# Gated attention and routed experts on one core: a new order of the steps ahead of the expert loop

## The reference

```
x = x + tanh(g_xattn) * attention(layernorm(x), ctx)
    # inside: layernorm of both again, q, k, v, softmax(q k^T / 16), v, Wo
n = layernorm(x)
w = softmax(n @ gate_w + gate_b)                # 8 experts
values, chosen = top_k(w, 2)
hidden = relu(n @ w1[e] + b1[e])                # 256 -> 1024
y[e] = hidden @ w2[e] + b2[e]                   # 1024 -> 256
x = x + tanh(g_ffn) * sum(values * y[chosen])
```

## Time and profile before

| what | value |
|---|---|
| median of 3 runs | 595.58 us (593.59 to 598.76) |
| the profiled execution, its own time | 594.17 us |
| its span, first to last instruction | 592.4 us |
| mean granted TensorE clock in it | 0.916 |
| TensorE busy | 513.9 us (87%) |
| ScalarE busy | 425.9 us (72%) |
| VectorE busy | 396.0 us (67%) |
| GpSimd busy | 276.6 us (47%) |

### The profile page before, as it was taken

One profiled execution on the slowest core, in us unless ns is written; L12 is line 12 of the kernel. 1 busy time (PEld: TensorE's weight loads), 2 busy tenths in 40 slices (PEclk: granted clock), 3 DMA queues, 4 the chain that ended last, 5 costly groups with the idle time before them and its releaser, 6 DMA issues.

```text
span 592.4 us, 15755 instructions
## 1 busy us (share of the span) xinstructions
PE 513.9 (87%) x4747; PEld 426.8 (72%) x4748; DVE 396.0 (67%) x1148; ACT 425.9 (72%) x1077; POOL 276.6 (47%) x292
## 2 busy tenths in 40 slices
PE   6958547566989998989999989999999999999991
PEld 3535325335878887768888877888999998999981
DVE  3359669787876666778666777876655665665660
ACT  2649688777766675867677756887888888888870
POOL 3110334843672223968732367885775233233232
PEclk8985575567999999999999999999999999999997
DMA  6999503233633224234332232534433332332221
GB/s 170 368 381 347 195 1 98 84 120 126 180 87 63 37 29 118 30 74 103 88 60 39 65 81 38 120 93 76 85 59 52 56 47 47 56 49 46 38 28 18
DMA packets 47633, 57.07 MB, mean 96 GB/s; under 512 B 6855, under 2 KB 43197, under 8 KB 47423
## 3 DMA queue, kind: packets, MB, share of 16 engines
q1 hardware_dynamic: 32223, 36.60, 20.3%
q0 software_dynamic: 14064, 18.55, 18.1%
q10 hardware_dynamic: 1264, 0.93, 0.5%
HBM read 33.19 MB, written 24.49 MB: 97 GB/s over the span
## 4 chain that ended last, share of the span: by engine, by line
PE 45%; DVE 10%; issue 8%; ACT 6%; POOL 3%; DMA 2%; ACTq 1%; DVEq 1%; SPq 0%; POOLq 0%
PE hid L1815 8%; PE hid L1819 7%; PE bank L1837 6%; PE bank L1839 6%; PE bank L1838 6%; PE hid L1818 4%; PE hid L1816 4%; ACT pool L924 3%; DVE pool L1468 3%; POOL xs L599 2%; PE bank L1796 2%; PE bank L1657 2%; PE bank L1675 1%; DVE pool L1483 1%; POOL out_dram L682 1%
## 5 line engine op out<-in xcount | busy, mean ns | idle before, releaser
L682 POOL DMA_INDIRECT out_dram<-pool,idx x71 | 115.4, 1625 | 196.1 <-DVE pool L1483 156.0
L924 ACT ACTIVATE pool<-hid,b1s 128x128 f32<-128x128 f32 x568 | 168.9, 374 | 12.7 <-PE hid L1819 4.7
L1815 PE MATMUL hid<-pool,w1h 128*128 128x256 f16 x568 | 155.4, 274 | 6.5 <-DVE pool L1468 3.5
L1837 PE MATMUL bank<-w2h,pool 128*128 x568 | 154.8, 273 | 4.3 <-issue 3.7
L1819 PE MATMUL hid<-pool,w1h 128*128 128x256 f16 x568 | 155.4, 274 | 0.0
L1839 PE MATMUL bank<-w2h,pool 128*128 x568 | 154.8, 273 | 0.0
L1838 PE MATMUL bank<-w2l,pool 128*128 x568 | 154.8, 273 | 0.0
L1468 DVE TENSOR_TENSOR pool<-hid,pool 128x512 f32<-128x512 f32 x142 | 96.5, 689 | 68.6 <-ACT pool L924 68.5
L1818 PE MATMUL hid<-pool,w1l 128*128 128x128 f16 x568 | 124.8, 220 | 0.0
L1816 PE MATMUL hid<-pool,w1l 128*128 128x128 f16 x568 | 124.8, 220 | 0.0
L933 ACT ACTIVATE pool<-pool 128x512 f16<-128x512 f32 x142 | 89.9, 637 | 36.0 <-DVE pool L1468 35.6
(11 more groups left out here) (276 smaller groups left out, 745.7 us busy)
## 6 DMA issues: line engine op xcount, KB each, us to landing
pool<-xs SPq DMA_DIRECT2D x71, 132.5 KB, 2.3
pool<-in_L_ffn_w_dram SPq DMA_DIRECT2D x8, 1024.0 KB, 8.3
xb<-in_x_dram SPq DMA_DIRECT2D x4, 1024.0 KB, 9.5
out_dram<-xb SPq DMA_DIRECT2D x4, 1024.0 KB, 5.2
w1h<-in_L_ffn_w_dram SPq DMA_DIRECT2D x2, 1024.0 KB, 10.7
w1l<-in_L_ffn_w_dram SPq DMA_DIRECT2D x2, 1024.0 KB, 11.4
w2h<-in_L_ffn_w_dram SPq DMA_DIRECT2D x2, 1024.0 KB, 13.5
w2l<-in_L_ffn_w_dram SPq DMA_DIRECT2D x2, 1024.0 KB, 12.6
```

Source lines behind the costliest of these rows:

```text
L682: g.indirect_dma_start(out=out_rows, out_offset=bass.IndirectOffsetOnAxis(ap=idx[s % U][:, 0:1], axis=0), in_=y2[s % 3], in_offset=None, c ...
L924: a.activation(hb[:, c * P:(c + 1) * P], bank[c // 2][:, (2 * (c % 2) + 1) * P:2 * (c % 2 + 1) * P], ACT.Identity, bias=b1s[:, ds(e * NH + ...
L1815: t.matmul(o, wh, xhl, start=True, stop=False)
L1837: t.matmul(o, hh[s % 2][:, hs], wh, start=c == 0, stop=False)
```

## The change

It alters the order of steps and which engine makes one low half; no new kind of operation is added. Experts are counted from 0 here.

- ScalarE, after image 0's tiles: `lo_tools(0)` goes ahead of both high halves of expert 2. `hi_part(3, 0)` and `gate_exp(0)` go ahead of `lo_copy(0)` and `square(4, 1)`. `hi_part(3, 1)` goes ahead of both squares of expert 5. The squares of expert 5 are written into `w1l` of experts 5 and 4, and `hi_part(3, 1)` no longer waits for them.
- VectorE, image 1: `scales_start(2)` moves from between the two low halves of expert 3 into turn k = 1 of the tiles, and `low_rows(0)` goes ahead of `scales(2)`.
- `by_pe` becomes (2, 6): TensorE makes the low half of w2 of expert 6 in place of expert 7, and the high halves of w2 of these two change places (`hi_turn`, and `hi_part(6, 1)` ahead of `hi_part(7, 1)`). VectorE's `lo_part(6, 1)`, ahead of `low_rows(1)`, is gone; `lo_part(7, 1)` comes in after `h_sum(0)`, and the wait for `s_lo` at 7 stands behind it.
- ScalarE, after `gate_exp(1)`: the order `lo_copy(1)`, `high_rows(1)`, `rows_T(0)`, `rows_T(1)` becomes `rows_T(0)`, `lo_copy(1)`, `rows_T(1)`, `high_rows(1)`, and the wait for `s_lo` at 7 moves behind `h_hi(0)`.
- TensorE: `position(1)` moves from ahead of the register loads for slots 0 and 1 to behind them.

```
--- before.py
+++ after.py
@@ -164,7 +164,7 @@
         raw_2 = [r[:, ND * H:] for r in raw] + [parked(w, e) for e in (E - 2 * EB, E - EB) for w in (w1l, w2l)]
         raw_of = [0, 1, 2, 3, 4, 5, 0, 1]
         raw_turn = [1, 1, 1, 1, 1, 1, 2, 2]
-        junk = [((w1l, e), (w2l, e)) for e in range(4)] + [((w1l, 3), (w2l, 3)), ((w2h, 3), (w2l, 3)),
+        junk = [((w1l, e), (w2l, e)) for e in range(4)] + [((w1l, 3), (w2l, 3)), ((w1l, 5), (w1l, 4)),
                                                           ((w1l, 5), (w2l, 5)), ((w1l, 6), (w1l, 7))]
         uq = sb("uq", [P, ND])
         st2 = sb("st2", [P, B, 6])
@@ -187,7 +187,7 @@
 
         diag = xT[0][:, 0, :]
         minus16 = xT[1][:, 0, 0:P // 2].bitcast(F16)
-        by_pe = (2, E - 1)
+        by_pe = (2, E - 2)
 
         st = [sb(f"st{b}", [P, T, 6]) for b in range(2)]
         mv = [sb(f"mv{b}", [P, T, 2]) for b in range(2)]
@@ -426,7 +426,7 @@
         def hi_turn(e, j):
             if e < E - EB:
                 return 2 * e + j + 1
-            return 2 * (E - EB) + ((1, 4), (2, 3))[e - (E - EB)][j]
+            return 2 * (E - EB) + ((1, 3), (2, 4))[e - (E - EB)][j]
 
         def tile_at(j):
             return [j] if 0 <= j < T else []
@@ -745,8 +745,8 @@
                     act.wait_ge(s_raw[k], raw_turn[e] * 32)
                     if e >= E - EB:
                         act.wait_ge(s_lo, e - 2)
-                elif e == 5:
-                    act.wait_ge(s_ssq, e)
+                    if e == 6:
+                        act.wait_ge(s_ssq, e)
                 w, n = junk[e][j]
                 a.activation(w[:, ds(n * ND * H, ND * H)], (raw_1, raw_2)[j][k], ACT.Square, accum_out=ssq[:, e, j:j + 1])
                 if j == 1:
@@ -757,8 +757,6 @@
             def hi_part(e, j):
                 k = raw_of[e]
                 act.wait_ge(s_scl, e // 2 + 1)
-                if (e, j) == (3, 1):
-                    act.wait_ge(s_ssq, 6)
                 if e >= E - 2 * EB:
                     act.wait_ge(s_lo, (3 if e < E - EB else 5) + j)
                 wh, src = ((w1h, raw_1[k]), (w2h, raw_2[k]))[j]
@@ -845,17 +843,17 @@
                 if k in (5, 6):
                     square(3, k - 5)
                 if k == 9:
+                    lo_tools(0)
                     hi_part(2, 0)
             hi_part(2, 1)
-            lo_tools(0)
             square(4, 0)
-            square(4, 1)
-            lo_copy(0)
             hi_part(3, 0)
             gate_exp(0)
+            lo_copy(0)
+            square(4, 1)
+            hi_part(3, 1)
             square(5, 0)
             square(5, 1)
-            hi_part(3, 1)
 
             for k in range(T + 2):
                 if k < T:
@@ -880,18 +878,14 @@
             lo_tools(1)
             hi_part(6, 0)
             hi_part(7, 0)
+            hi_part(6, 1)
             hi_part(7, 1)
-            hi_part(6, 1)
             act.wait_ge(s_nmr, 1)
             act.wait_ge(s_outd, 2 * 16)
             for i in range(T // 2):
                 x = xb[1][:, i, 0:D]
                 a.activation(x, x, ACT.Identity, scale=rs[1][:, i:i + 1], bias=nmr[:, i:i + 1]).then_inc(s_xn, 1)
             gate_exp(1)
-            lo_copy(1)
-            high_rows(1, 0, T)
-
-            act.wait_ge(s_lo1, 1)
 
             def attention_start(s):
                 for b, j in attention_steps(s):
@@ -939,11 +933,14 @@
                     act.wait_ge(g_y2, s - 1)
                 a.activation(y1[s % 2], summed, ACT.Copy, scale=q[s % U][:, 0:1]).then_inc(g_y1, 1)
 
+            act.wait_ge(s_lo1, 1)
             rows_T(0)
+            lo_copy(1)
             rows_T(1)
-            act.wait_ge(s_lo, E - 1)
+            high_rows(1, 0, T)
             h_bias(0)
             h_hi(0)
+            act.wait_ge(s_lo, E - 1)
             for s in range(S):
                 attention_start(s)
                 if s + 2 < S:
@@ -1364,14 +1361,14 @@
             places(0)
             rows_norm_2(0, T // 2, T)
             lo_part(3, 0)
-            scales_start(2)
             lo_part(3, 1)
 
             for k in range(T + 5):
                 tile_of(1, k)
                 if k == 1:
+                    scales_start(2)
+                    low_rows(0, 0, T)
                     scales(2)
-                    low_rows(0, 0, T)
                 if k in (2, 3):
                     lo_part(4, k - 2)
                 if k == 4:
@@ -1396,7 +1393,6 @@
             lo_part(7, 0)
             gates(1)
             places(1)
-            lo_part(6, 1)
             low_rows(1, 0, T)
 
             def attention_start(s):
@@ -1483,8 +1479,9 @@
                 v.scalar_tensor_tensor(y2[s % 3], b2s[:, ds(e * D, D)], q[s % U][:, 1:2], y1[s % 2], ALU.mult,
                                        ALU.add).then_inc(g_y2, 1)
 
+            h_sum(0)
+            lo_part(E - 1, 1)
             dve.wait_ge(s_lo, E - 1)
-            h_sum(0)
             e = {0: expert_of(0), 1: expert_of(1)}
             gate(0, e[0])
             gate(1, e[1])
@@ -1735,7 +1732,6 @@
                     norms(3)
             lo_raw(1)
             lo_rest(1)
-            position(1)
 
             def attention_mid(s):
                 for b, j in attention_steps(s):
@@ -1845,6 +1841,7 @@
             load_at(1)
             load_adr(0, 0)
             load_adr(0, 2 * NH)
+            position(1)
             turn_rows(0)
             turn_rows(1)
             pe.wait_ge(s_lo1, EB)
```

8 lines of the change are left out of this document (3 added, 5 removed).

## The result

The changed kernel took **597.28 us** (median of 20 runs, 595.47 to 602.11), the kernel before on the same chip 594.08 us (20 runs, 592.1 to 599.26). The ratio is 1.0049, with a 95% interval from 1.0025 to 1.0072: slower by some 3 us, and within the one per cent of no change to which the prediction gave 0.91. The profiled execution took 595.47 us, the shortest of the 20, with a span of 593.7, at a mean clock of 0.917. Ratios leave out executions over 1.5% above the fastest of the same kernel, so that a ratio need not be the quotient of the medians beside it; e7b's profiled execution is such a one.

A forecast was written before the change was run, and what follows sets the result against it. TensorE was taken as full from about 170 us, with VectorE's chain setting the loop's start. y_sum(0) 3.5 us later, gains included, on the profiled 594.17 gave 597.7; 598.0 was forecast, allowing for the base, range 594.0 to 601.5.

The forecast's parts named there:

- The forecast case: The main case: y_sum(0)'s 3.5 us delay reaches the end, 596.8 to 599.7 on the profiled run's base; chance 0.62.
- First place: Image 0 to image 1: VectorE's 1.5 us gain isn't kept; 0.35 us is left, between 0 and 1.5.
- if the tiles of image 1 start before 88: One of three signs that would show the prediction wrong; VectorE was forecast to reach image 1's first scores at 89.2.
- Second place, gain: Slot 0's rows turned at 133.8, not 135.70, and h_sum(0) ending at 142.75, not 144.2: 1.4 us sooner.
- Second place, cost: lo_part(7, 1) on VectorE delays h_low(0) and the b2 load; y_sum(0) comes 3.5 us later, between 2.6 and 5.5.
- this alone sends `h_sum(1)` to some 148.8, by 1.1: On VectorE, h_low(0), 1.4 us late and ending at 148.4, by itself makes h_sum(1) 1.1 us later.
- b2 wait: VectorE waits ahead of h_sum(1) for the b2 load, issued at 145.1 and landing at 150.6 (149.7 to 152.6).
- A clock of 1.0 from 145 to 160: Expected in the profile after: a clock of 1.0 from 145 to 160 us.
- rival B: TensorE's clock falls to half in two gaps at the loop's start: 601.1, or 603 with slow b2 landing; chance 0.08.
- No idle time takes it in: VectorE's chain can't absorb the delay and TensorE is full from about 170 us: 3.5 us reach the end.
- A: Rival: the first place's gain is passed on and the b2 load isn't last to come: 593.1 us; chance 0.16.
- C: Rival: the b2 wait ends before h_low(0), or idle time in slots 1 to 4 absorbs it: 595.3; chance 0.14.

The follow-up runs named there:

- e7b: The changed kernel with lo_part(7, 1) ahead of low_rows(1), the b2 wait just ahead of y_sum(0), scales(2) ahead of low_rows(0), measured again: 619.89 us, ratio 0.9958.
- e3: The kernel before with only the first place changed (ScalarE's order after image 0, the squares' places, scales_start(2) and low_rows(0)): 617.38 us, ratio 1.0014.
- e1b: The changed kernel with VectorE's wait for the b2 load moved to just ahead of y_sum(0), second measurement: 595.95 us, ratio 1.0041.
- e5: The kernel before with the b2 load issued behind the rows of slot 4 in SyncE's queue: 602.73 us, ratio 1.014.
- e7: The changed kernel with lo_part(7, 1) ahead of low_rows(1), the b2 wait just ahead of y_sum(0), scales(2) ahead of low_rows(0): 593.59 us, ratio 0.9988.
- e2: The changed kernel with lo_part(7, 1) moved ahead of low_rows(1), where VectorE waits for high_rows(1): 616.39 us, ratio 1.0001.
- e2b: The changed kernel with lo_part(7, 1) moved ahead of low_rows(1), second measurement: 595.93 us, ratio 1.0039.

## Why the prediction was right

The forecast case held: +3.5 us were forecast on the profiled execution, and 2.9 (ratio), 3.2 (medians) and 3.1 (trace) came out, towards the lower end of its 2.6 to 5.5. The 598.0 us itself, given for a base between 594.17 and 595.58, lies 0.7 above the measured 597.28, whose base was 594.08. Step by step, with 1.78 us added to the times of after:

```
step                                   forecast   after + 1.78
norms(2)                                 86.9        85.9
VectorE at image 1's first score         89.2        87.8
hi_part(4, 0)                            93.3        93.4
lo_part(4, 0)                            95.1        95.4
turn of slot 0                          133.8       133.3
hidden(0)                               136.9       136.4
end of h_sum(0)                         142.75      143.1
h_low(0)                                147.0       147.4
b2 load, issued and landed              145.1 150.6 145.4 150.8
h_sum(1)                                151.5       151.7
y_sum(0)                                154.2       154.3
end of the span                         595.9       595.5
```

- **First place, right for half of the reason.** A gain of 0.35 us was booked (0 to 1.5), and none came: e3 turns slot 0 as late as before. `norms(2)` came 0.5 sooner, not 0.5 later, and the first scores reached VectorE 2.9 us sooner (the earlier trace rows against 86.05 + 1.78). By its own sign, "if the tiles of image 1 start before 88" (they did, by 0.2 us, at 87.8), the prediction was wrong about this stretch. All of the gain went between there and the release of `hi_part(4, 0)`. The step had `low_rows(0)`, 2.28 us, and lacked GpSimd's root. Moved behind the first score, `scales_start(2)` has the root run beside `low_rows(0)`, and it took 3.31 us, not 1.34 as before; VectorE waited another 1.24 us for it. That the release came at 93.4 as forecast (93.3) was luck: the first score 1.4 us too early, the root too late. GpSimd in after, and then before:

```profile
86.84 3.31 POOL L588 TENSOR_TENSOR nrm<-nrm,half 128x6 f32<-128x6 f32 x1 [10.22 <-DVE nrm L983]
```

```profile
88.09 1.34 POOL L588 TENSOR_TENSOR nrm<-nrm,half 128x6 f32<-128x6 f32 x1 [9.19 <-DVE nrm L986]
```

- **Second place, gain:** 1.4 us booked at the end of `h_sum(0)`, 1.1 found (144.25 against 143.1). `hidden(0)` started 2.1 us sooner than before, but took 0.8 longer at half clock, which the prediction didn't count.
- **Second place, cost: right in its sum, wrong in its split.** `h_low(0)` came 1.85 us later (1.4 booked) and b2 landed within 0.2 of the forecast. The step that failed is "this alone sends `h_sum(1)` to some 148.8, by 1.1". In e1b, where the b2 wait is gone, `h_low(0)` is 2.4 us later than before and `h_sum(1)` 2.3: ScalarE's `h_bias(1)` waits for `h_low(0)`, so it follows nearly one to one (in after, `h_low(0)` is 1.85 us late and not 2.4). And `y_sum(0)` is 3.3 later, since it needs `output(0)` too, which there starts only with `h_low(0)`, took 1.3 us longer, and which the prediction didn't follow. The b2 wait, priced at 2.4 of the 3.5, adds 0.25 to 0.8. It does end last, as forecast, and that is why the times agree; but it is nearly covered. So the number hardly rests on the term that most of it was built on: without that wait it would have come out 0.25 to 0.8 us lower, and that it fitted all the same says little for the price of 2.4.
- **"A clock of 1.0 from 145 to 160"** was wrong: 0.67 and 0.50 from 146 to 150. This is rival B's mechanism, but in the changed kernel it wasn't what `y_sum(0)` waited for, and without the b2 wait it costs at most 0.9 us there, not 3.4. It hit `output(0)` alone, because the second gap, ahead of `hidden(2)`, never opened: `output(0)` ran right up to it.
- **No idle time takes it in**, and the shift reaches the end nearly 1:1: 3.56 us at `y_sum(0)`, 3.45 at `y_sum(1)`, 3.1 at the end; in e5, 6.3 became 8.0. Rivals A and C are out: A since the first place gives nothing by itself (e3), C since even without the b2 wait (e1b) the rest ends 2.9 us later than before.

## What to carry to other kernels

When a step moves behind another on an in-order queue, look for the idle time that it leaves as well as for the queue that it now holds: the same 2.34 us cost 4.6 us at `y_sum(0)` behind `h_sum(0)`, and nothing 6 us sooner, where the engine stood waiting. When a late step feeds two engines, price both paths to the point where they meet; taking away the wait that shows in the trace gives back only the difference between them. And measure shifts of a few microseconds in the trace from an event that the change can't touch, since the run times of this kernel scatter by more than the shift; but take more than one trace of each, since here the same code differed by 0.7 us in one place.

## What the runs showed of the hardware

**The stretch ahead of the change has two lengths.** The windows view of two executions from 15 to 30 us, where their code is the same (before, then e7):

```profile
15.00:30.00 15.00, 13.27 (x59) 8.06 (x57) 4.95 (x27) 10.08 (x21) 1.67 (x1) 0.99 1.08 368
```

```profile
15.00:30.00 15.00, 14.82 (x34) 8.11 (x35) 4.12 (x23) 6.16 (x13) 1.67 (x1) 0.54 1.08 368
```

The first has a clock of 0.99 and does 59 matmuls, the second 0.54 and 34. `scales(1)` ends at 65.6 to 67.9 us in the one case, at 73.2 or 73.3 in the other (before's code in e5 among them), with one execution at 71.7. In e7 the rest took 523.5 us, so its profiled execution, 598.52 us and the longest of its 12 runs, would have been near 592.6 with the 67.4 us of before ahead of it. What decides between the two I didn't find.

**Chips differ in places.** The same kernel before took 594, 616 and 622 us. In e2 and e2b, the same code, all is alike to 0.13 us up to `h_low(0)` (77.19 and 77.22); then VectorE waits in e2 as follows (0.34 us in e2b):

```profile
151.86 0.69 DVE L1465 TENSOR_TENSOR pool<-hid,pool 128x512 f32<-128x512 f32 x1 [4.85 <-ACT pool L918]
```

and `y_sum(0)` is 4.5 us later. On such a chip something else ends last from slot 0 on and hides an effect of 3 us. What it is stays open: ScalarE's `h_bias(1)` stands still twice in e2, for 2.00 and 2.29 us, and the trace names no engine of this core for it.

**GpSimd's small operations took longer beside VectorE's big ones where VectorE's had begun first:** the root above, 1.34 to 3.31 us, beside `low_rows(0)`, begun 0.17 us ahead of it, and a scatter of after that took 3.01 us at 141.43 beside `lo_part(7, 1)`, begun at 141.26, against 0.96 to 1.06 for its neighbours. The same operation of GpSimd (L625), in before and then in after, shows both orders:

```profile
70.14 3.67 POOL L625 TENSOR_TENSOR rs<-vv,neghalf 128x8 f32<-128x8 f32 x1 [3.89 <-DVE vv L1261]
```

```profile
68.37 1.64 POOL L625 TENSOR_TENSOR rs<-vv,neghalf 128x8 f32<-128x8 f32 x1 [3.89 <-DVE vv L1258]
```

In before VectorE's `lo_part(2, 0)` had begun at 69.97; in after it began at 68.38, 0.01 us behind, and lasted as long (2.35 us). For the time of this kernel only the root mattered, as far as these runs show.
